# A transformer block on one core: eight PSUM banks and early feed-forward tiles in the epilogue, an earlier norm, halved stores and four banks of maxima in the prologue

## Chip, cores and metric

The kernel runs on one NeuronCore of one Trainium2 chip. The metric is the device time of one execution in microseconds; lower is better. Names used below: PE is TensorE, ACT is ScalarE, DVE is VectorE, POOL is GpSimd, SP is the SyncE queue that issues nearly all DMAs. A bank is one of the eight 128x512 fp32 accumulators in PSUM.

## What is computed

Eight batches of 1024 tokens with 256 channels go through one adaptive-norm transformer block: causal attention with 16 heads of 16 channels, then a feed-forward layer with a router over four low-rank experts (top two). Cut to what matters:

```
mod = (silu(c) @ wmod).reshape(8, 6, 1, 256);  sa, ca, ga, sb, cb, gb = mod[:, 0..5]
h = layernorm(x) * (1 + ca) + sa
x = x + ga * attention(h)          # q, k, v, o: x @ w.T + x @ a.T @ b.T / 16
h = layernorm(x) * (1 + cb) + sb
w, top = router(h)                 # softmax of h @ Wg.T + bg, the two best of four experts
hid_e = relu(h @ Wi.T + low_rank_e(h))              # 1024 hidden channels
x = x + gb * sum over the two experts of w_e * (hid_e @ Wo.T)
```

## The kernel before

Each engine walks one common plan, a list of steps in one order (`walk`, line 352), and issues its own part of each step. So the plan's order is the order of every engine's queue, and of SP's DMAs. The plan has phases: `prologue_plan` (line 258: weights turned, batch 0 normalised and projected, maxima of its first head group), eight bodies (`body_plan`: attention of batch i, with the feed-forward work of batch i-1 and the projections of batch i+1 laid between), and `epilogue_plan` (line 277: output projection, second norm, route and feed-forward of the last batch, with no attention beside it).

PSUM is divided by use: three `dense` banks, two `mxs` banks for the maxima, two `st` banks for scores, one `ov` bank for the attention output. Steps in `DENSE` take the dense banks in turn.

The steps that matter here:

- `su i`: setup. `su 0` to `su 8` make the modulation and the four projection matrices; `su 3` on DVE is `setup_gates` (line 1141); `su 9` to `su 18` turn the feed-forward weights.
- `ls1`/`ln1` and `ls2`/`ln2`: statistics (line 1159) and normalisation (lines 1181 to 1194, then 1294) of the first and the second norm, all on DVE. `t1`/`t2`: PE turns the result, ACT applies the modulation (line 1085).
- `pa`/`pj`: a projection of q or k in two matmul steps; ACT, DVE and POOL split it into three bf16 parts (lines 1094, 1331, 1334, 751). `va`/`vp`/`vs`: values and their store.
- `ps ot`: SP stores the parts of q and k of one half of the channels to DRAM (line 636). `rs slot half g`: SP loads one head group's stack from there, 13 small DMAs (lines 646, 651). It waits for `ps`.
- `mx`: PE makes scores for the row maxima in an `mxs` bank (lines 880, 884), DVE reduces it (line 1314); PE waits for the bank used two steps before. The prologue has 39 `mx` steps, four beside each `su`. `ms`, `nm`: the maxima are finished, turned by PE (line 972), copied by ACT (line 1109), and put into the stack by DMA (line 672); then the first scores `qk` (line 896) can start.
- `oa`/`op`: output projection (line 849), gated by DVE (line 1353), added to x by POOL (line 763).
- `rt`, `rx`, `ro`: route: logits, turn, `lg` copy by DVE (line 1359), then a chain of small DVE instructions (lines 1220 to 1262). `mt`, `rb` (lines 967, 861): its results are turned by PE and copied by ACT to `low_st` (1105) and `ratio_b` (1107).
- `fa`, `fx`, `fb`: one of 16 feed-forward tiles (half of the tokens, eighth of the hidden channels): base product (two 128x512 fp32 products on line 855, the first in `fa`, the second in `fx`), low-rank part of the best expert (line 922), relu by ACT (line 1079), then in the same bank the difference to the second expert (line 928), DVE (line 1368, two buffers `second`), POOL adds the two into `hid` (line 756). `wa`/`w`: the output product over `hid` (lines 1001, 936), DVE (1377), POOL (769), SP stores the rows. `w` of the first token tile waits for the last tiles of `hid`.

In the epilogue before, the order of the tiles is fa, fx, fa, fx, fb, fb for each pair.

## Time and profile before

| | us |
|---|---|
| median of 3 runs | 1964.28 (1963.49 to 1966.62) |
| the profiled execution | 1965.01 |
| its span in the trace | 1963.3 |
| PE busy | 1801.6 (92% of the span) |
| DVE busy | 1239.0 (63%) |
| ACT busy | 939.6 (48%) |
| POOL busy | 530.5 (27%) |

How to read it: the span is what the trace covers; 1.7 us of the execution lie outside it. Times of rows count from the span's start. The body runs from about 101 to 1850 us; what is before it is the prologue, what is behind it the epilogue. A busy PE is not a PE at full rate: its clock has two levels, and the column PEclk gives the granted one as a share of 2.4 GHz.

### The profile page before, as it was taken

The page shows a single profiled execution, that of the slowest core. Times are in us where ns is not written, and L with a number is a line of the kernel's source. Part 1 is how long each engine was busy: PE and PEld are TensorE (multiplying, and loading weights), DVE is VectorE, ACT ScalarE, POOL GpSimd, SP SyncE. Part 2 cuts the span into 40 slices and gives each one's busy share as a digit, 9 for nine tenths or more (in the row PEclk, how much of TensorE's full clock was granted, in tenths as well). Part 3 has the DMA queues.
Part 4 walks back from the last instruction along what each step waited for, and adds up shares of the span by engine and source line. Part 5 has one row for each costly group of instructions (what it writes and reads, how often), then busy time and mean ns, then how long its engine had stood idle before and what let it go on. Part 6 is the DMA issues. An engine that isn't in the chain of part 4 may idle for free. (4 is left out here: it accounts for less than half of the span.)

```text
span 1963.3 us, 31621 instructions
## 1 busy us (share of the span) xinstructions
PE 1801.6 (92%) x10868; PEld 943.5 (48%) x10868; DVE 1239.0 (63%) x2681; ACT 939.6 (48%) x1701; POOL 530.5 (27%) x833
## 2 busy tenths in 40 slices
PE   7689879999989999899999999899999999799868
PEld 5334335454544555444554545445554545344535
DVE  3666677757686577666676576765777565863131
ACT  2145555544455445545455445554455454554320
POOL 2012112233223222233222232232222332133313
PEclk9579899999999999999999999999999999899979
DMA  7523243213322223223222233223222132120000
GB/s 177 145 50 87 51 87 83 70 40 78 85 60 71 56 64 87 70 38 92 63 71 70 40 85 70 72 58 82 47 60 79 31 88 63 39 39 25 25 1 22
DMA packets 249862, 128.69 MB, mean 66 GB/s; under 512 B 158214, under 2 KB 244834, under 8 KB 249708
## 3 DMA queue, kind: packets, MB, share of 16 engines
q1 hardware_dynamic: 245564, 125.61, 26.6%
q10 hardware_dynamic: 4144, 1.07, 0.4%
q8 instruction: 92, 1.51, 0.4%
q14 instruction: 62, 0.51, 0.1%
HBM read 83.06 MB, written 41.97 MB: 64 GB/s over the span
## 5 line engine op out<-in xcount | busy, mean ns | idle before, releaser
L1049 ACT ACTIVATE probs<-st 128x512 f32<-128x512 f32 (+1 forms) x1216 | 674.8, 576 | 705.2 <-PE st L896 703.1
L1314 DVE TENSOR_REDUCE negm<-mxs 128x1 f32<-128x384 f32 (+4 forms) x736 | 446.6, 617 | 243.3 <-PE mxs L884 239.1
L896 PE MATMUL st<-q_st,k_st 98*128 98x512 bf16 (+3 forms) x1536 | 452.3, 333 | 25.5 <-ACT probs L1049 18.3
L880 PE MATMUL mxs<-k_st,q_st 96*128 96x512 bf16 (+3 forms) x1280 | 408.1, 329 | 47.0 <-DVE negm_left L1314 26.7
L1314 DVE TENSOR_REDUCE negm_left<-mxs 128x1 f32<-128x512 f32 x512 | 345.2, 687 | 144.6 <-PE mxs L880 142.2
L911 PE MATMUL ov<-probs,v_g 128*32 128x512 f32 (+3 forms) x3072 | 333.2, 506 | 1.2 <-POOL probs L743 1.1
L880 PEld LDWEIGHTS mxs<-k_st,q_st 96*128 96x128 bf16 x1280 | 124.0, 98 | 300.8 <-DVE negm_left L1314 98.6
L855 PE MATMUL dense<-c_t,wi_t 128*128 128x512 f32 x512 | 263.9, 601 | 3.3 <-ACT ratio_b L1107 2.4
L756 POOL TENSOR_TENSOR hid<-hid,second 128x512 f32<-128x512 f32 x128 | 161.7, 1266 | 305.6 <-DVE second L1368 305.6
L896 PEld LDWEIGHTS st<-q_st,k_st 98*128 98x128 bf16 x1536 | 142.3, 99 | 169.1 <-ACT probs L1049 66.1
L740 POOL TENSOR_TENSOR fence<-fence 128x1 f32<-128x1 f32 x256 | 50.2, 196 | 613.8 <-ACT probs L1049 613.7
L884 PE MATMUL mxs<-k_st,q_st 128*128 128x128 bf16 x1024 | 188.8, 225 | 14.9 <-DMA k_st<-k_parts_scratch 9.1
L1368 DVE SCALAR_TENSOR_TENSOR second<-dense,ratio_b 128x512 f32<-128x512 f32 x128 | 88.3, 690 | 135.8 <-PE dense L928 135.8
L743 POOL TENSOR_SCALAR_AFFINE_SELECT probs<-probs 128x512 f32<-128x512 f32 x256 | 162.5, 635 | 0.0
L884 PEld LDWEIGHTS mxs<-k_st,q_st 128*128 128x128 bf16 x1024 | 93.6, 100 | 90.6 <-issue 25.3
L841 PE MATMUL dense<-h_t,w_t 128*128 128x512 f32 x256 | 134.1, 613 | 1.1 <-ACT v_rows L1097 0.8
L911 PEld LDWEIGHTS ov<-probs,v_g 128*32 128x32 f32 x3072 | 61.0, 108 | 132.7 <-issue 98.8
L1079 ACT ACTIVATE hid<-dense 128x512 f32<-128x512 f32 x128 | 76.4, 597 | 96.0 <-PE dense L922 94.3
L936 PE MATMUL dense<-wo_t,hid 128*128 128x256 f32 x512 | 121.3, 379 | 0.0
L1001 PE MATMUL dense<-wo_t,hid 128*128 128x256 f32 x512 | 121.0, 379 | 0.0
L769 POOL TENSOR_TENSOR ob<-ob,x 128x256 f32<-128x256 f32 x64 | 47.1, 737 | 237.3 <-DVE ob L1377 237.3
L855 PEld LDWEIGHTS dense<-c_t,wi_t 128*128 128x128 f32 x512 | 89.3, 191 | 33.3 <-issue 20.1
(165 smaller groups left out, 1696.4 us busy)
## 6 DMA issues: line engine op xcount, KB each, us to landing
q_st<-q_parts_scratch SPq DMA_DIRECT2D x384, 64.0 KB
k_st<-k_parts_scratch SPq DMA_DIRECT2D x384, 64.0 KB
q_parts_scratch<-q_part SPq DMA_DIRECT2D x16, 768.0 KB, 3.3
k_parts_scratch<-k_part SPq DMA_DIRECT2D x16, 768.0 KB, 5.2
xin<-in_L_attn_x SPq DMA_DIRECT2D x8, 1024.0 KB, 5.9
values_scratch<-v_rows SPq DMA_DIRECT2D x32, 256.0 KB, 2.1
v_g<-values_scratch SPq DMA_DIRECT2D x128, 64.0 KB, 3.9
x<-in_L_attn_x SPq DMA_DIRECT2D x16, 512.0 KB, 4.3
```

The costliest lines, as they stand in the source:

```text
L743: nc.gpsimd.affine_select(out=tri, in_=tri, compare_op=ALU.is_ge, fill=0.0, base=0, pattern=[[0, HG], [1, P]], channel_multiplier=-1).then ...
L756: nc.gpsimd.tensor_tensor(hid[:, ft, :], hid[:, ft, :], second[:, ft % 2, :], ALU.add).then_inc(hid_ready, 1)
L841: return nc.tensor.matmul(db[:, :], w_t[:, WNAMES.index(which), k, ot * P:(ot + 1) * P], h_t[:, k, half * HB:(half + 1) * HB], start=(k == ...
L855: nc.tensor.matmul(db[:, :], wi_t[:, k, ft * P:(ft + 1) * P], c_t[:, k, half * HB:(half + 1) * HB], start=(k == 0), stop=False)
L880: last = nc.tensor.matmul(mxs[:, bank_m, j * n:j * n + left], q_st[0:KS, slot, h0 + j, qt * P:(qt + 1) * P], k_st[0:KS, slot, h0 + j, k0:k ...
L884: last = nc.tensor.matmul(mxs[:, bank_m, j * n + left:(j + 1) * n], q_st[:, slot, h0 + j, qt * P:(qt + 1) * P], k_st[:, slot, h0 + j, qt * ...
L896: last = nc.tensor.matmul(st[:, score_bank(ch, kt, h0), j * n:(j + 1) * n], k_st[0:KS + 2, slot, h0 + j, kt * P:(kt + 1) * P], q_st[0:KS + ...
L911: last = nc.tensor.matmul(ov[32 * j:32 * j + 32, HB - n:HB], v_g[:, slot, kt, j, :], probs[:, par, j, 0:n], start=(kt == 0), stop=(kt == 4 ...
L936: last = nc.tensor.matmul(db[:, 0:D], hid[:, ft, t * P:(t + 1) * P], wo_t[:, ft, :], start=False, stop=(ft == FT - 1))
L1001: nc.tensor.matmul(db[:, 0:D], hid[:, ft, t * P:(t + 1) * P], wo_t[:, ft, :], start=(ft == 0), stop=False)
L1049: nc.scalar.activation(probs[:, par, h0:h0 + heads, 0:n], st[:, score_bank(ch, kt, h0), 0:heads * n].rearrange("p (j q) -> p j q", q=n), A ...
L1314: nc.vector.tensor_reduce(dst[:, h0:h0 + heads], src, axis=AX.X, op=ALU.max, negate=True).then_inc(max_free, 1)
```

## The change

In the epilogue:

- The dense steps rotate over all eight banks instead of three; the first step waits until the last scores, maxima and output are read.
- For the last batch `fa` makes both base products, and five tiles' `fa` (`EARLY_TILES`) stand behind the route's steps and ahead of `mt`. After them each tile's `fa` follows the `fb` of the tile five before it, `fb` follows the `fx` of the tile two after it, and the first `fa` steps of the second token half stand ahead of the first half's `wa`.
- `ls2 i` follows `op i` directly, instead of all four following all four.

In the prologue:

- `ls1` and `ln1` follow `su 0`; the scale for `t1` is copied in `setup_gates` and ACT waits for that copy.
- `ps` is halved along the tokens everywhere (in the bodies the two halves follow each other). In the prologue the first half is stored as soon as its two projections are split, and the loads of the first group (`rs 0 0`, `rs 0 1`) come ahead of values 2 and 3 and their stores.
- `mx` uses four banks (`mxs` and `st`) instead of two.
- The second `ps` stands behind `nm 0` instead of ahead of it.

```diff
+    plan = [("su", 0)] + chain_steps(("ls1", "ln1")) + [("su", i) for i in range(1, N_PROJECTION_SETUP)]
+    plan += [("t1", i) for i in range(4)] + [("xin",)]
     values = [opened("va", i) for i in range(4)]
-    plan += values[0] + values[1] + pj[0] + [("ps", 0, 0)]
-    plan += values[2] + values[3] + [("rs", g, half, g) for g in range(2) for half in range(2)] + [("vg", 0)]
+    plan += values[0] + values[1]
+    for half in range(2):
+        plan += pj[0][4 * half:4 * half + 4] + [("ps", 0, 0, half)]
+    plan += [("rs", 0, half, 0) for half in range(2)] + values[2] + values[3]
+    plan += [("rs", 1, half, 1) for half in range(2)] + [("vg", 0)]
...
-    plan += [("ms",), ("ps", 1, 0), ("nm", 0)] + score_steps(0, *UNITS[0])
+    plan += [("ms",), ("nm", 0), ("ps", 1, 0, 0), ("ps", 1, 0, 1)] + score_steps(0, *UNITS[0])
...
 def epilogue_plan():
-    plan += [s for i in range(4) for s in opened("oa", i)]
-    plan += chain_steps(("ls2", "ln2")) + [("t2", i) for i in range(4)] + [("rt",), ("rx",)] + chain_steps(("ro",))
+    for i in range(4):
+        plan += opened("oa", i) + [("ls2", i)]
+    plan += chain_steps(("ln2",)) + [("t2", i) for i in range(4)] + [("rt",), ("rx",)] + chain_steps(("ro",))
+    tiles = [(half, ft) for half in range(2) for ft in range(8)]
+    plan += [("fa", *t) for t in tiles[:EARLY_TILES]]
     plan += [("mt", v) for v in range(2)] + [("rb", half) for half in range(2)]
     for half in range(2):
-        for ft in range(0, 8, 2):
-            plan += [(name, half, ft + i) for i in range(2) for name in ("fa", "fx")]
-            plan += [("fb", half, ft + i) for i in range(2)]
+        of_half = tiles[8 * half:8 * half + 8]
+        for i, t in enumerate(of_half):
+            plan.append(("fx", *t))
+            n = 8 * half + i - 2
+            if i >= 2:
+                plan.append(("fb", *tiles[n]))
+            if i >= 2 and n + EARLY_TILES < 16:
+                plan.append(("fa", *tiles[n + EARLY_TILES]))
+        for n in (8 * half + 6, 8 * half + 7):
+            plan.append(("fb", *tiles[n]))
+            if n + EARLY_TILES < 16:
+                plan.append(("fa", *tiles[n + EARLY_TILES]))
         plan += [s for t in range(4) for s in opened("wa", half, t)]
+EARLY_TILES = 5
+EPILOGUE_BANKS = 8
...
+        banks = [dense[:, i, :] for i in range(DENSE_BANKS)] + [mxs[:, i, :] for i in range(MAX_BANKS)]
+        banks += [st[:, i, :] for i in range(SCORE_BANKS)] + [ov[:, :]]
+        def max_room(it):
+            spare = [st[:, i, :] for i in range(SCORE_BANKS)] if it < 0 else []
+            return [mxs[:, i, :] for i in range(MAX_BANKS)] + spare
...
-                    ot, later = a
+                    ot, later, half = a
+                    cols = slice(half * HB, (half + 1) * HB)
                     for dst, src in ((q_d, q_part), (k_d, k_part)):
-                        sp.dma_start(dst[ot], src[:, ot, :, :]).then_inc(parts_out[ot], 16)
+                        sp.dma_start(dst[ot, :, :, cols], src[:, ot, :, cols]).then_inc(parts_out[ot][half], 16)
...
-                    sp.wait_ge(parts_out[ot], done(f"ps{ot}") * (2 * 16))
+                    sp.wait_ge(parts_out[ot][half], done(f"ps{ot}{half}") * (2 * 16))
...
-                    after(pe, max_free, done("mx") - MAX_BANKS + 1)
+                    room = max_room(it)
+                    out = room[done("mx") % len(room)]
+                    after(pe, max_free, done("mx") - len(room) + 1)
...
                     elif kind == "fa":
                         hidden(db, 0, *a)
+                        if it == NB:
+                            hidden(db, 1, *a)
                         return
```

## Rows read from the trace of the kernel before

**Rows 1.** Busy time of each engine by stage, then granted clock, DMA share, GB/s
```profile
62.66:94.40 31.74, 26.17 (x110) 13.73 (x110) 24.89 (x41) 5.31 (x9) 1.15 (x1) 0.50 0.56 129
...
100.89:1850.47 1749.58, 1645.82 (x10211) 843.15 (x10211) 1156.16 (x2471) 898.34 (x1633) 481.14 (x764) 0.98 0.27 64
...
1861.94:1887.64 25.70, 6.51 (x35) 4.14 (x35) 15.65 (x67) 3.71 (x6) 1.72 (x2) 0.60 0.00 0
```

**Rows 2.** Timeline of the prologue ahead of the first maxima: start, duration, engine, line
```profile
30.76 1.50 PE L861 MATMUL dense<-ident,xin 128*128 128x128 f32 x12 [0.66 <-DVE xin L1294]
...
43.66 1.15 POOL L751 TENSOR_TENSOR k_part<-rest,k_part 128x512 bf16<-128x512 f32 x1 [0.55 <-DVE k_part L1334]
...
48.66 0.43 SPq L636 DMA_DIRECT2D k_parts_scratch<-k_part  x1
...
53.56 0.73 SPq L646 DMA_DIRECT2D q_st<-blank_scratch  x1
...
62.66 0.61 PE L884 MATMUL mxs<-k_st,q_st 128*128 128x128 bf16 x4 [6.70 <-DMA k_st<-k_parts_scratch]
```

**Rows 3.** The first load of `xin`, issued at 1.74 us: from issue to landing
```profile
DMA to landing us min/median/max: 9.1/9.1/9.1
```

**Rows 4.** DVE's longest group of waits in the maxima: total us, times, longest
```profile
DVE negm L1314 <- PE mxs L884: 8.2, 7, 5.1
```

**Rows 5.** Timeline of the first scores
```profile
100.89 1.03 PE L896 MATMUL st<-q_st,k_st 98*128 98x512 bf16 x2 [4.70 <-DMA q_st<-m_row]
```

**Rows 6.** SP's timeline in the first body: a store, and the next load
```profile
179.76 0.43 SPq L636 DMA_DIRECT2D k_parts_scratch<-k_part  x1
187.82 0.62 SPq L646 DMA_DIRECT2D q_st<-blank_scratch  x1
```

**Rows 7.** Timeline of the epilogue, output projection and second norm
```profile
1856.87 0.69 DVE L1353 TENSOR_TENSOR second<-dense,gates_b 128x512 f32<-128x512 f32 x1 [5.02 <-PE dense L849]
1857.71 1.27 POOL L763 TENSOR_TENSOR x<-x,second 128x512 f32<-128x512 f32 x1 [8.60 <-DVE second L1353]
...
1864.16 2.71 DVE L1159 BATCH_NORM_STATS2 stats<-x 128x6 f32<-128x256 f32 x8 [1.44 <-POOL x L763]
```

**Rows 8.** Timeline of the epilogue around the route
```profile
1879.93 0.39 DVE L1359 COPY lg<-dense 128x80 f32<-128x80 f32 x2 [7.04 <-PE dense L991]
...
1887.64 1.91 PE L967 MATMUL dense<-ident_b,low_w 128*96 128x128 bf16 x16 [7.75 <-DVE low_w L1262]
1888.74 1.92 ACT L1105 COPY low_st<-dense 96x1024 bf16<-96x1024 bf16 x2 [7.43 <-PE dense L967]
...
1890.55 1.25 ACT L1107 COPY ratio_b<-dense 128x512 f32<-128x512 f32 x2
```

**Rows 9.** Short stretches where the granted clock falls and rises, columns as in rows 1
```profile
58.00:58.50 0.50, 0.00 (x0) 0.00 (x0) 0.24 (x2) 0.00 (x0) 0.00 (x0) 0.50 0.49 148
...
1887.60:1891.00 3.40, 3.36 (x24) 3.25 (x24) 0.00 (x0) 2.26 (x3) 0.00 (x0) 0.51 0.00 0
1891.00:1894.40 3.40, 2.63 (x9) 1.17 (x8) 0.00 (x0) 0.98 (x3) 0.00 (x0) 1.00 0.02 5
```

**Rows 10.** The chain that ended last, one pair of tiles: start, duration
```profile
1930.92 1.72 PE dense L855 x4
1932.64 0.22 PE dense L922
...
1934.83 0.61 ACT hid L1079
```

**Rows 11.** Timeline of the same pair of tiles, and of the last output rows
```profile
1935.49 0.39 PE L928 MATMUL dense<-low_st,b_stack 96*128 96x512 bf16 x1 [0.47 <-ACT hid L1079]
...
1935.82 2.49 POOL L756 TENSOR_TENSOR hid<-hid,second 128x512 f32<-128x512 f32 x2 [2.46 <-DVE second L1368]
1935.91 0.69 DVE L1368 SCALAR_TENSOR_TENSOR second<-dense,ratio_b 128x512 f32<-128x512 f32 x1 [0.17 <-PE dense L928]
...
1959.81 0.48 DVE L1377 SCALAR_TENSOR_TENSOR ob<-dense,rs_,gates_b 128x256 f32<-128x256 f32 x1 [2.97 <-PE dense L936]
```

74 lines of the change are left out of this document (44 added, 30 removed).

## Prediction, made before the changed kernel was run

> **What bounds the kernel now.** I read the busy time by stage first. In the body PE is busy for 1645.8 of 1749.6 us at a granted clock of 0.98 [rows 1]: it is the bound there, and the change removes no PE work from it. So whatever the change brings must come from the 100 us ahead of the body and the 113 us behind it. Four stretches there leave PE waiting. First, PE stands 6.7 us until the first stack has landed [rows 2]. Second, the maxima take 31.74 us, in which DVE works for 24.89 and PE runs at clock 0.50 [rows 1]. Third, between the output projection and the route's result PE works 6.5 of 25.7 us [rows 1]. Fourth, the feed-forward of the last batch, some 68 us, is a chain of PE with one exposed relu per pair of tiles [rows 10, 11].
>
> **Prologue, start of the loads.** Before, the loads began at 53.56, because SP stored q and k only after both halves were split (issue of k at 48.66) and waited for the landing [rows 2]. Now the first half can be stored when its k is split, 43.66 + 1.15 = 44.8. The early norm takes some more: the load of xin landed at 1.74 + 9.1 = 10.8 [rows 3], the norm's DVE work is 8.7 us (the epilogue's twin of it runs from 1864.16 to 1872.9), so it ends near 20, long before the turns at 29.5. What it saves is only the wait of 0.66 [rows 2] less what ACT then can't follow: I take 0.5. So the first half is issued by 45.1. But SP still has the second half's store in its queue ahead of the loads: that waits for POOL as before, 0.5 earlier, and its two issues end at 49.09 - 0.5 = 48.6. The first half has landed by then if it takes 3.5 us, and by 50.0 if it takes as long as the whole took from 48.66 (4.9, up to 53.56). I take 48.6, as half the bytes move: loads 4.9 us earlier (bound 3.5). From the first load to the first max it was 62.66 - 53.56 = 9.1 us, 13 issues and a landing, and stays so: first max at 57.7. PE's own work before it ends at 55.5 and doesn't hold it. The stores of values 2 and 3 go behind these loads on SP; they are needed by the gather `vg`, whose queue turn comes after all four loads, near 76, and by the product at about 96. Cost nothing.
>
> **Prologue, the maxima.** With two banks PE may be one step ahead of DVE, so each `su` between them (four turns, 0.86 us at the half clock) starves DVE: its largest group of waits is 8.2 us, of which 5.1 is the start [rows 4], and 31.74 - 24.89 = 6.9 us of the stage are without DVE [rows 1]. With four banks, a replay of the order by hand (a 512-column product 0.43 us of PE, a reduce 0.67, 0.54 or 0.40 of DVE, DVE 0.3 behind PE) never starves DVE after the start. The stage is then DVE's 24.9 us plus 0.7 at the start plus 0.6 for gaps, 26.2: 5.5 us shorter. The bounds: DVE without any gap gives 6.1. If the second half's stack comes late (its loads end at 61.4, land at 64.1, PE wants it at about 64.6) or PE at 0.50 is the slower (its 26.2 busy us [rows 1], run in series, with the start), 3. Behind the maxima, turn, copy and the row's DMA are as before; the first scores stay bound to that DMA [rows 5]. The second store now stands behind it, lands near 95 and is first loaded in unit 7, some 40 us later. Prologue: -4.9 - 5.5 = **-10.4 us**, between -12 and -6.5. The body starts on the same work, just earlier.
>
> **Body.** 14 stores become pairs of halves: two more issues each of 0.34 to 0.43 us, 0.8 us of SP, and runs of 1 KB where they were longer. The load behind such a store began 7.6 us after its issue ended (180.19 to 187.82), against a landing of about 5 from its start [rows 2, 6]: some 3 us of slack hide it. Taken as 0; below nothing is excluded only for the store itself, since where PE's clock dips fall in the body moves with the start; I allow +-2 for that.
>
> **Epilogue, the second norm.** Here the change costs. DVE's queue is in order: `ls2 i` waits for POOL's sum, and the next `op` stands behind it. One link is 0.69 (DVE) + 0.15 + 1.27 (POOL) + 0.03 + 2.71/4 (statistics) = 2.84 us [rows 7]. Four make 11.4 from 1856.87, so statistics end at 1868.2, against 1864.16 + 2.71 = 1866.9 before: **+1.4 us**, and everything up to the route is that much later. Eight banks give nothing back here, since no dense step waited for a bank.
>
> **Epilogue, the filled gap.** `fa` of tile 0 needs all banks read, so it follows the `lg` copy: 1880.32 + 0.1 + 1.4 = 1881.8. The route's last result comes at 1887.6 + 1.4 = 1889.0 [rows 8]. Five tiles at 1.72 us [rows 10] are 8.6 us at full clock. But PE stands at 0.50 here, and rose 3.3 us after it had become continuously busy [rows 9]: 3.3 us at half speed add 1.7, twice that 3.3. I take 2.5: `fa` ends at 1881.8 + 11.1 = 1892.9, 3.9 us after the route, so the turns start later than before by 5.3. From their start, ACT is the chain: 0.6 for the first turn at full clock, copies of 1.92 and 1.25 [rows 8], 0.1: the first `fx` starts at 1896.8, against 1890.55 + 1.25 + 0.1 [rows 8] + 1.72 = 1893.7 before: **+3.1 us** (this holds the +1.4). At once at full clock it would be +0.6, at half clock for all five (17.2 us) +9.2.
>
> **Epilogue, from the first `fx` to the end.** Before: 1893.7 to 1959.81, 66.1 us [rows 11]. It held 15 base products, now 11: -4 x 1.72 = -6.9. One pair of tiles showed relu 0.61 and its handover, with PE idle 0.47 and 0.17 more of refilling [rows 10, 11]: 8 x 0.64 = -5.1. What comes back: `fb 0` of each half stands too close to its relu (2 x 0.42), and at the end of the second half no base products are left between the tiles, so PE needs 0.44 per tile (two low-rank products at 0.22 [rows 10]), ACT 0.61, DVE 0.69 and POOL 1.25 (2.49 for two) [rows 11]. There PE waits 0.4 twice for relus; the last five tiles queue at POOL, and the first `w` waits 0.15 + 0.76 + 1.62 for `hid`. Together +4.1. Sum **-7.9 us**. In the first half base products of the second lie in between, and POOL keeps up. The tail behind the last `w` is unchanged. Epilogue: +3.1 - 7.9 = **-4.8**.
>
> **The sum.** -10.4 - 4.8 = -15.2. Against the profiled execution 1965.0 - 15.2 = 1949.8; against the median, which lies 0.7 below it, **1949.1 us**.
>
> **The rivals.** (A) The clock takes the fill back. PE keeps 0.50 through all five `fa`: +6.1, 1955.2. For it: in the 25.7 us around the norm and the route PE works in pieces and gets 0.60 on average [rows 1]. Against: its `fa` are gapless, as the work was before the rise. A milder form is that the clock falls between the last `fa` and the first `fx`: 1.7 us of turns and 2.2 us of waiting; PE is at 0.50 from 58.0, and its last instruction before the 6.7 us of waiting for the stack [rows 2] had ended at 62.66 - 6.70 = 55.96, so it fell after 2.0 us [rows 9]. It would then stay low some 3.3 us and cost 1.7: 1950.8. The Trainium skill speaks for this form ("TensorE: Matmul & The Clock Gate", Part 4, PE-mode transpose): transposes do not count as PE-busy, so the whole 3.9 us would be idle to the clock. The trace speaks against that page: from 1887.6 to 1891 PE did turns only, 3.36 of 3.40 us, and the clock rose at the end of it [rows 9]. (B) The prologue gives half: the loads start when they did, since the halved stores share the queues and land late, or the maxima become bound by PE or by the second half's stack. 1949.1 + 4.9 = 1954.0 or + 2.5 = 1951.6; both 1956.5. For it: the slack at the second half's stack is 0.5 us. (C) Slower: the halved stores in the body. Each of the 14 loses its slack when it lands over 7.6 us after the issue, and then PE, the bound, waits for the loads behind it. At 9 us each costs 1.4: +19.6, 1968.7, slower. It decides from a landing of about 9 us; against it, the bytes are the same and SP is idle for long. (D) More than forecast: fill at full clock at once (-2.5) and an earlier rise in the first body, 1945.
>
> **Chances and range.** Forecast 0.60 (1946 to 1953); A 0.12; B 0.15; C 0.04; D 0.06; the prologue or the fill not doing what it says while the other does, near 1960, 0.03. Low end: D with a shorter prologue, 1944.5. High end: B whole, 1956.5; that leaves out under 2 in 10. About 0.2% (3.9 us) is what a measurement of this kernel tells from no change: faster 0.91, within it 0.05, slower 0.04.
>
> **What would show it.** Right: first load near 48.6 and first max near 57.7; no reduce waiting over 0.3 us after the start and `ms` near 84; first scores near 90.5; statistics of the second norm 11.4 us behind the first `op`; five tiles of line-855 products between the `lg` copy and the turns, the first two at half rate; no relu wait inside the first half; POOL back to back at the end of the second half, with PE waiting for it some 2.5 us at the first `w`. Wrong: the stage of the maxima near 30 us; a granted clock of 0.50 over all `fa`; a body whose length differs from 1749.6 by over 2 us; loads that wait for halved stores.

## The result, and the profile of the changed kernel

The changed kernel took 1948.01 us (median; 1945.34 to 1949.17 in four runs) beside 1965.45 us for the kernel before on the same chip. The ratio is 0.9895 with a 95% interval of 0.987 to 0.9921. Measured twice more, it came to 0.9905 (0.9883 to 0.9927) and 0.9894 (0.9871 to 0.9917). So the change is faster by some 1.0%, where 15.2 us or 0.8% were forecast, and the time fell in the range. All three intervals lie below 1. The profiled execution took 1949.06 us with a span of 1947.3, that is 16.0 us less span.

The stages first, as in rows 1: the maxima, the body, the stretch from the end of norm 2's statistics to the route's end, and the last piece of the five early tiles.

```profile
57.70:82.17 24.47, 18.58 (x110) 10.71 (x110) 23.20 (x41) 5.32 (x9) 1.15 (x1) 0.79 0.70 129
88.50:1837.70 1749.20, 1646.19 (x10210) 844.25 (x10211) 1155.78 (x2471) 898.92 (x1633) 481.08 (x764) 0.98 0.28 65
1859.25:1878.85 19.60, 12.46 (x47) 7.05 (x48) 12.20 (x58) 3.71 (x6) 0.00 (x0) 0.68 0.00 0
1878.85:1882.10 3.25, 3.25 (x9) 1.27 (x8) 0.00 (x0) 0.00 (x0) 0.00 (x0) 1.00 0.00 0
```

The body is what it was: 1749.20 us against 1749.58, PE busy 1646.19 against 1645.82 [rows 1]. The maxima are 7.3 us shorter and DVE now works in 23.20 of 24.47 us. Everything that was gained lies ahead of the first scores (12.4 us) and behind the body (3.2 us in this profile). The rest of the 16.0 is the body's 0.4.

Next the timeline of the prologue (start, duration, engine, line), the rows that answer to rows 2 and rows 5. L920 is the first maximum, L932 the first score.

```profile
28.05 2.18 PE L893 MATMUL dense<-ident,xin 128*128 128x128 f32 x16
...
43.52 0.62 SPq L668 DMA_DIRECT2D k_parts_scratch<-k_part  x1
...
46.26 0.51 SPq L668 DMA_DIRECT2D q_parts_scratch<-q_part  x1
46.82 0.63 SPq L668 DMA_DIRECT2D k_parts_scratch<-k_part  x1
47.56 0.73 SPq L678 DMA_DIRECT2D q_st<-blank_scratch  x1
...
52.40 1.83 SPq L683 DMA_DIRECT2D q_st<-q_parts_scratch  x1
...
57.70 0.40 PE L920 MATMUL mxs<-k_st,q_st 128*128 128x128 bf16 x4 [3.75 <-DMA k_st<-k_parts_scratch]
...
88.50 1.04 PE L932 MATMUL st<-q_st,k_st 98*128 98x512 bf16 x2 [4.67 <-DMA q_st<-m_row]
```

The first half's store ends its issue at 44.14 and the loads begin at 47.56, 0.11 us behind the second half's last issue. The first half had landed just before. This is the view of `k_parts_scratch` from 40 to 60 us; the longest, 4.0 us from the issue at 43.52, is the first half's k:

```profile
DMA to landing us min/median/max: 3.4/3.7/4.0
```

So it landed at 47.5, and here landing and queue let the loads go at practically the same moment. In the two other profiles of this kernel it had landed 0.04 and 0.11 us before the last issue ended. The turns of norm 1 no longer have a gap in front of them. One of the small load issues took 1.83 us where its neighbours take 0.43.

The waits in the stage of the maxima (total, times, longest), which answer to rows 4: DVE waits for 2.0 us at the start and once more for 0.6, at 66.8 us.

```profile
DVE negm L1360 <- PE mxs L920: 2.0, 1, 2.0
DVE negm_left L1360 <- PE mxs L916: 0.6, 1, 0.6
```

Then the epilogue: one link of the second norm, the base products behind the `lg` copy, the turns of `mt`, and the end of the second half.

```profile
1850.78 0.67 DVE L1399 TENSOR_TENSOR second<-dense,gates_b 128x512 f32<-128x512 f32 x1
1851.59 1.26 POOL L795 TENSOR_TENSOR x<-x,second 128x512 f32<-128x512 f32 x1 [1.52 <-DVE second L1399]
1852.89 0.75 DVE L1204 BATCH_NORM_STATS2 stats<-x 128x6 f32<-128x256 f32 x2 [1.44 <-POOL x L795]
1853.56 0.67 DVE L1399 TENSOR_TENSOR second<-dense,gates_b 128x512 f32<-128x512 f32 x1
...
1871.75 5.36 PE L887 MATMUL dense<-c_t,wi_t 128*128 128x512 f32 x8 [0.48 <-DVE lg L1405]
1876.95 3.60 PE L887 MATMUL mxs<-c_t,wi_t 128*128 128x512 f32 x8
1880.38 1.88 PE L887 MATMUL st<-c_t,wi_t 128*128 128x512 f32 x4
1882.10 0.61 PE L1007 MATMUL st<-ident_b,low_w 128*96 128x128 bf16 x8
...
1926.07 6.16 POOL L788 TENSOR_TENSOR hid<-hid,second 128x512 f32<-128x512 f32 x5 [0.89 <-DVE second L1414]
...
1927.48 1.97 PE L1043 MATMUL mxs<-wo_t,hid 128*128 128x256 f32 x8 [0.37 <-POOL hid L788]
1929.85 1.13 PE L976 MATMUL mxs<-wo_t,hid 128*128 128x256 f32 x4 [0.40 <-POOL hid L788]
1932.29 1.13 PE L976 MATMUL mxs<-wo_t,hid 128*128 128x256 f32 x4 [1.31 <-POOL hid L788]
```

DVE's queue shows the new chain: a statistics step waits 1.44 us for POOL, and the next `op` starts only as it ends, every 2.78 us. The base products fill the route; the first eight take 5.36 us where the next eight take 3.60, because the clock rose inside them. At the end five adds stand back to back at POOL and PE waits 0.37 + 0.40 + 1.31 = 2.08 us for them.

### The profile page after: what moved, and what is told of

It is laid out like the page before. It is cut to its first block, busy times and chain, and to the rows that moved or that the text cites. A ratio compares the mean times of both kernels' runs of the same rounds, so it can differ in the third digit from the quotient of the medians.

```text
span 1947.3 us, 31669 instructions
## 1 busy us (share of the span) xinstructions
PE 1795.9 (92%) x10868; PEld 943.3 (48%) x10868; DVE 1236.8 (64%) x2681; ACT 939.5 (48%) x1701; POOL 530.6 (27%) x833
## 3 DMA queue, kind: packets, MB, share of 16 engines
q10 hardware_dynamic: 4144, 1.07, 0.4%
## 4 chain that ended last, share of the span: by engine, by line
PE 75%; DVE 14%; ACT 4%; issue 3%; SPq 2%; DMA 1%; POOL 1%; POOLq 0%; DVEq 0%; ACTq 0%
PE ov L947 12%; PE st L932 10%; PE dense L887 10%; PE mxs L916 9%; PE dense L873 5%; PE dense L1043 5%; PE dense L976 5%; PE dense L881 4%; DVE negm L1360 4%; PE dense L893 3%; DVE negm_left L1360 3%; PE mxs L920 2%; PE dense L968 2%; ACT probs L1091 1%; SPq L683 1%
## 5 line engine op out<-in xcount | busy, mean ns | idle before, releaser
L1360 DVE TENSOR_REDUCE negm<-mxs 128x1 f32<-128x384 f32 (+4 forms) x725 | 439.7, 617 | 238.2 <-PE mxs L920 234.5
L932 PE MATMUL st<-q_st,k_st 98*128 98x512 bf16 (+3 forms) x1536 | 454.2, 334 | 25.7 <-ACT probs L1091 17.3
L916 PE MATMUL mxs<-k_st,q_st 96*128 96x384 bf16 (+2 forms) x1261 | 397.6, 325 | 44.1 <-DVE negm_left L1360 26.2
L1360 DVE TENSOR_REDUCE negm_left<-mxs 128x1 f32<-128x512 f32 x504 | 339.5, 686 | 140.7 <-PE mxs L916 138.8
L887 PE MATMUL dense<-c_t,wi_t 128*128 128x512 f32 x480 | 250.4, 606 | 3.0 <-ACT ratio_b L1151 1.7
L932 PEld LDWEIGHTS st<-q_st,k_st 98*128 98x128 bf16 x1536 | 142.2, 99 | 169.4 <-ACT probs L1091 65.5
L920 PE MATMUL mxs<-k_st,q_st 128*128 128x128 bf16 x1009 | 184.4, 224 | 11.3 <-DMA k_st<-k_parts_scratch 5.5
L1414 DVE SCALAR_TENSOR_TENSOR second<-dense,ratio_b 128x512 f32<-128x512 f32 x120 | 82.8, 690 | 117.1 <-PE dense L968 115.2
L920 PEld LDWEIGHTS mxs<-k_st,q_st 128*128 128x128 bf16 x1009 | 91.4, 99 | 87.6 <-issue 25.7
L801 POOL TENSOR_TENSOR ob<-ob,x 128x256 f32<-128x256 f32 x64 | 47.1, 737 | 239.3 <-DVE ob L1423 239.3
L1043 PE MATMUL dense<-wo_t,hid 128*128 128x256 f32 x464 | 109.6, 379 | 0.0
L976 PE MATMUL dense<-wo_t,hid 128*128 128x256 f32 x464 | 109.6, 379 | 0.0
L1121 ACT ACTIVATE hid<-dense 128x512 f32<-128x512 f32 x120 | 71.3, 597 | 76.7 <-PE dense L962 75.0
L887 PEld LDWEIGHTS dense<-c_t,wi_t 128*128 128x128 f32 x480 | 84.0, 192 | 28.1 <-issue 14.0
```

The costliest lines, as they stand in the source:

```text
L887: nc.tensor.matmul(db[:, :], wi_t[:, k, ft * P:(ft + 1) * P], c_t[:, k, half * HB:(half + 1) * HB], start=(k == 0), stop=False)
L916: last = nc.tensor.matmul(out[:, j * n:j * n + left], q_st[0:KS, slot, h0 + j, qt * P:(qt + 1) * P], k_st[0:KS, slot, h0 + j, k0:k0 + left ...
L920: last = nc.tensor.matmul(out[:, j * n + left:(j + 1) * n], q_st[:, slot, h0 + j, qt * P:(qt + 1) * P], k_st[:, slot, h0 + j, qt * P:(qt + ...
L932: last = nc.tensor.matmul(st[:, score_bank(ch, kt, h0), j * n:(j + 1) * n], k_st[0:KS + 2, slot, h0 + j, kt * P:(kt + 1) * P], q_st[0:KS + ...
L976: last = nc.tensor.matmul(db[:, 0:D], hid[:, ft, t * P:(t + 1) * P], wo_t[:, ft, :], start=False, stop=(ft == FT - 1))
L1043: nc.tensor.matmul(db[:, 0:D], hid[:, ft, t * P:(t + 1) * P], wo_t[:, ft, :], start=(ft == 0), stop=False)
```

## Experiments

The stages in the profiles of the kernel before and of the changed kernel, profiled three times, in us (starts are of the first instruction; "ce" is the epilogue's first turn; "last DVE step" is the start of DVE's last instruction):

| | before | changed | again | once more |
|---|---|---|---|---|
| first value projection | 33.64 | 31.63 | 31.14 | 31.41 |
| first load | 53.56 | 47.56 | 47.07 | 47.34 |
| load to first max | 9.11 | 10.15 | 10.06 | 10.65 |
| maxima | 31.73 | 24.47 | 23.76 | 24.43 |
| first scores | 100.89 | 88.50 | 86.95 | 88.88 |
| body | 1749.58 | 1749.20 | 1750.04 | 1748.33 |
| ce to first `op` | 6.40 | 10.26 | 6.46 | 10.26 |
| first `op` to end of statistics | 10.01 | 11.24 | 11.24 | 11.25 |
| statistics to end of `lg` | 13.44 | 12.49 | 12.50 | 12.49 |
| route's end to turns | 0.15 | 3.28 | 3.31 | 3.27 |
| turns to first `fx` | 6.09 | 3.79 | 3.79 | 3.79 |
| first `fx` to last DVE step | 66.07 | 57.93 | 57.93 | 57.92 |

### One half of the change at a time

`e1_epilogue_only` has the old order of the prologue, with two banks for the maxima, and the new epilogue; its stores stay halved, both halves next to each other. `e2_prologue_only` is the reverse.

```diff
 # e1_epilogue_only
-    plan = [("su", 0)] + chain_steps(("ls1", "ln1")) + [("su", i) for i in range(1, N_PROJECTION_SETUP)]
+    plan = [("su", i) for i in range(N_PROJECTION_SETUP)]
+    plan += chain_steps(("ls1", "ln1")) + [("t1", i) for i in range(4)] + [("xin",)]
...
-            spare = [st[:, i, :] for i in range(SCORE_BANKS)] if it < 0 else []
+            spare = []
...
 # e2_prologue_only
-    plan += [("fa", *t) for t in tiles[:EARLY_TILES]]
...
-    phase(epilogue_plan(), batches, EPILOGUE_BANKS)
+    phase(epilogue_plan(), batches)
```

> The changed epilogue with the prologue's order, two banks of maxima and the late norm as before; stores stay halved, both halves next to each other. Theory 1 (the two ends add up, each worth what its stages show): first load near 53 to 54, first max to the end of the maxima 31 to 32 us, and from the first turn of the epilogue (ce) to the end 109.6 us if the clock dips there again, near 106 if it does not, against 112.8 before. Time 3 to 7 us below the kernel before, 1958 to 1962. Theory 2 (the halved stores alone start the prologue's loads earlier, whatever the order): first load below 52. Theory 3 (the gain at the end is spent on the longer norm and the late turns): from ce to the end 112 or more, time as before.

> The changed prologue with the epilogue as before (three banks, pairs of tiles, statistics after all four gated rows). Theory 1: first scores near 88.5 to 90.5 against 100.9, body 1749 to 1750 long, from ce to the end 112.8; time 10.4 to 12.4 below before, 1953 to 1955. Theory 2 (an earlier start is lost again in the body, whose pace is set by something else): body longer than 1752, time above 1956.

Measured: the epilogue alone 1960.98 us, ratio 0.9965 (0.995 to 0.9979); the prologue alone 1954.52 us, 0.9927 (0.9907 to 0.9946), beside 1968.89 for before. That is 7.9 and 14.4 us. The two together give 1.08%, the whole change 0.95 to 1.06%: within the intervals the halves add up. The prologue carries about two thirds, as forecast. Both medians are where Theory 1 had them. The profiles agree: `e1` has its first load at 54.01 and 107.33 us from ce to the end, against 112.81 before; `e2` has its first scores at 88.28 and a body of 1750.01 us. Only its epilogue took 116.72 us where 112.8 were expected, 3.8 of it at its first turns (last section). Theory 2 of `e1` (halving alone starts the loads earlier) is out: there the first half's k had landed at 52.6, but SP was still issuing the stores of values until 53.9.

### The statistics behind the projection

```diff
-    for i in range(4):
-        plan += opened("oa", i) + [("ls2", i)]
-    plan += chain_steps(("ln2",)) + [("t2", i) for i in range(4)] + ...
+    plan += [s for i in range(4) for s in opened("oa", i)]
+    plan += chain_steps(("ls2", "ln2")) + [("t2", i) for i in range(4)] + ...
```

> The changed kernel with one edit undone: the statistics of the second norm come after all four gated rows again. Theory 1 (statistics between the rows make DVE wait for POOL four times in series): from the first gated row to the last statistics 10.0 us instead of 11.2, and all behind it 1.2 us earlier; time 1 to 1.5 below the changed kernel. Rival (the oa rows or PE are the later ones, so the order does not matter): no difference in that stretch. Rival 2 (statistics between rows save, as meant): the stretch becomes longer than 11.2.

> The changed kernel once more, for the phase of TensorE's clock. Theory 1 (the half clock at the epilogue's first turns, 3.9 us longer from ce to the first gated row than before, is chance): here that stretch (10.3 us in the first profile, 6.4 before) may come out at 6.4 again, and the setup turns L834 at 273 or 421 ns each. Rival (the change causes it): 10.3 again. Ratio to before 0.987 to 0.992.

Measured: 1947.65 us, 0.9894 (0.9874 to 0.9914), beside 1947.63 for the changed kernel. (That one took 6.46 us from ce to the first `op` this time, so its Theory 1, chance, held; see the last section.) Its stage shrank to 10.00 us as it had been before (11.24 in the changed kernel): in this stage the new order costs 1.24 us, and DVE's statistics now run as one block.

```profile
1848.72 1.26 POOL L794 TENSOR_TENSOR x<-x,second 128x512 f32<-128x512 f32 x1 [0.46 <-DVE second L1398]
1850.01 2.71 DVE L1203 BATCH_NORM_STATS2 stats<-x 128x6 f32<-128x256 f32 x8 [1.44 <-POOL x L794]
```

But the total didn't move; the 1 to 1.5 us that were expected didn't come. (The profiled execution, 1944.06 us, is the shortest of its six, by a body of 1745.42 us, and isn't a measure of the edit.) The windows of this kernel from the statistics to the `lg` copy, and from there on:

```profile
1852.72:1866.33 13.61, 6.47 (x34) 4.10 (x34) 5.92 (x34) 3.48 (x5) 0.00 (x0) 0.50 0.00 1
1866.33:1876.00 9.67, 9.61 (x18) 4.33 (x19) 6.33 (x26) 0.23 (x1) 0.00 (x0) 0.79 0.00 0
```

The clock stayed at 0.50 through the turns and logits (13.61 us against 12.50), and the turns of `mt` began 3.63 us after the route instead of 3.31. So 1.24 us came off and 1.11 + 0.32 came back through the clock. From the first `op` to the first `fx` this kernel takes 38.16 us and the changed one 37.92. That is no accident of this one profile: the three kernels with the statistics in one block and no products added (before, `e2`, `e3`) have 13.44, 13.45 and 13.61 us from the statistics to the end of `lg`, while all seven profiles with the statistics between the rows and no products added (the changed kernel three times, `e1`, `e4`, `e5`, `e6`) have 12.36 to 12.50. In those the logits already run at the high clock and take 1.07 us instead of 1.93. Whether the order itself brings the clock's rise forward isn't shown, since no run moves the clock alone.

### Two banks for the maxima, and the stores in one piece

```diff
 # e4_two_max_banks
-            spare = [st[:, i, :] for i in range(SCORE_BANKS)] if it < 0 else []
+            spare = []
 # e5_stores_together
-    for half in range(2):
-        plan += pj[0][4 * half:4 * half + 4] + [("ps", 0, 0, half)]
+    plan += pj[0] + [("ps", 0, 0, 0), ("ps", 0, 0, 1)]
```

> The changed kernel with two banks for the prologue's maxima instead of four. Theory 1 (PE may be only one step ahead, so each setup step starves DVE): first max to end of maxima back to 31 to 32 us at the half clock, 28 if part of it runs at full clock, against 24.5 and 23.8 in the two profiles of the changed kernel; DVE waits for PE some 5 us more. Rival (the stage became short because the clock stayed full at its start, since the stack came earlier): 24 to 26 us here too.

> The changed kernel with both halves of the first store put behind all four projections of the first half of the channels, loads directly behind them. Theory 1 (the loads' start is the second half's store issue, because the landing of the first half is hidden behind it): loads start when the second half has landed, so from the first value projection to the first load 19.5 to 20 us instead of 15.9, first max 3.5 to 4 later, time 3.5 to 4 above the changed kernel. Rival (SP's queue order alone, the loads ahead of the values' stores, made the gain): 16 to 17 us.

Measured with two banks: 1955.97 us, 0.994 (0.9922 to 0.9959). The stage of the maxima:

```profile
58.33:90.06 31.73, 26.17 (x110) 13.72 (x110) 24.88 (x41) 5.31 (x9) 1.15 (x1) 0.50 0.50 100
```

It is the stage of before to 0.02 us in each engine [rows 1], as Theory 1 had it; the rival (24 to 26 us here too) is out. The profiled execution is the longest of the ten (1966.47 us), but for reasons behind this stage: its body took 1758.73 us. The two banks more are worth 31.73 - 24.47 = 7.3 us and the other edits of the prologue nothing here. The granted clock was higher with four banks too (0.79 for 0.50), and PE's busy time follows it (18.58 against 26.17). How much of the 7.3 belongs to that isn't separated, since all three profiles with two banks (before, `e1`, `e4`) had 0.50 throughout. With four banks the granted clock lay between 0.74 and 0.86 and the stage between 23.8 and 24.5 us, and DVE was busy for 23.20 of the 24.47 us: in that range PE's rate hardly sets the length.

Measured with the stores together: 1952.4 us, 0.9929 (0.9905 to 0.9952). SP's queue in this kernel:

```profile
48.15 0.65 SPq L667 DMA_DIRECT2D q_parts_scratch<-q_part  x1
48.84 1.09 SPq L667 DMA_DIRECT2D k_parts_scratch<-k_part  x1
50.94 0.73 SPq L677 DMA_DIRECT2D q_st<-blank_scratch  x1
```

From the first value projection to the first load it was 18.77 us, against 15.93 in the changed kernel in every profile. So the early store of the first half is worth 2.84 us at the load's start. Only 1.0 us of SP's queue is idle here (49.93 to 50.94). The wait is for the first half, whose k was issued at 47.49 and landed at 50.92, 3.4 us later, where the whole of before had taken 4.9. The second half landed only at 53.19. So Theory 1 was wrong in what the loads wait for, and 18.77 lies between its 19.5 to 20 and the rival's 16 to 17. Against the kernel before (19.92) the other 1.15 us is mostly the faster landing of a half. It doesn't come by halving alone: `e1`, with the values' stores in front of the loads, has 20.13.

### Three tiles open in the second half

The order lets the second half keep only three tiles' base products ahead, so that two base products more lie among the last tiles.

```diff
     for half in range(2):
...
-            if i >= 2 and n + EARLY_TILES < 16:
-                plan.append(("fa", *tiles[n + EARLY_TILES]))
...
+        ahead = EARLY_TILES if half == 0 else LATE_AHEAD
+        limit = 8 + LATE_AHEAD if half == 0 else 16
...
+            if name == "fb" and begun < limit and begun <= n + ahead:
+                plan.append(("fa", *tiles[begun]))
+                begun += 1
...
 EARLY_TILES = 5
+LATE_AHEAD = 3
```

> The changed kernel with a shorter lead in the second token half: only three of its tiles' base products are made during the first half, the other five lie between its tiles. Same PE work. Theory 1 (the last tiles queue at POOL, 1.25 us each, because no base product lies between them): PE's waits for hid and relu at the first output product fall from about 3.1 to 1.7 us, first fx to last output row 57.0 us against 57.9. Rival (PE waits there for something else): 57.9 or more.

Measured: 1946.18 us, 0.9892 (0.9865 to 0.9919); first `fx` to last DVE step 57.16 us, against 57.93. POOL's block and the wait of the first `w`:

```profile
1926.52 3.71 POOL L794 TENSOR_TENSOR hid<-hid,second 128x512 f32<-128x512 f32 x3 [0.89 <-DVE second L1420]
1930.29 1.13 PE L982 MATMUL st<-wo_t,hid 128*128 128x256 f32 x4 [1.12 <-POOL hid L794]
```

Three adds in a block instead of five, and PE waits once for 1.12 us instead of three times for 2.08. In return PE now waits 0.55 us at the first half's `w`, where two tiles begun early had stood before. The stretch is 0.8 us shorter, as expected (57.0 for 57.9), so the queue at POOL behind the last tiles is shown as a cost; the medians (1946.18 here, 1947.6 to 1948.5 for the changed kernel) can't tell.

### Extra products ahead of norm 2's turns

```diff
+WARM = 11
...
+                    if it == NB and step == ("t2", 0):
+                        after(pe, dense_free[bank], done(f"bank{bank}"))
+                        for i in range(WARM):
+                            nc.tensor.matmul(db[:, :], w_t[:, 0, i % KC, 0:P], h_t[:, i % KC, 0:HB],
+                                             start=True, stop=True)
```

> The changed kernel with eleven 128x512 fp32 products added on PE, whose results nobody reads, while DVE normalises ahead of t2. Theory 1 (the half clock in t2, the route and the five early fa costs some 3 us): the clock stays at 1.0 from the gated rows to the end; last statistics to the lg copy 11.5 us against 12.5 (13.5 where the clock rose late); route's end to the turns 1.5 us against 3.3; turns to first fx 3.8 as before; together 2.5 to 3 us shorter from the last statistics to the first fx (was 26.7). Rival (a mere DVE and ACT chain, PE's rate does not matter): 26 to 27. If the products outlast the norm, the first stretch grows instead.

Measured: 1944.84 us, 0.9886 (0.9863 to 0.9908). From the statistics to the first `fx` it took 24.2 us, against 26.7 in the changed kernel: 11.67 us to the end of `lg` instead of 12.49, and the turns 1.62 us after the route instead of 3.28. So far Theory 1 held. Four windows from the turns of `mt` on:

```profile
1879.32:1883.12 3.80, 2.16 (x26) 1.71 (x25) 0.00 (x0) 2.89 (x4) 0.00 (x0) 1.00 0.00 0
1883.12:1884.90 1.78, 1.52 (x6) 0.64 (x7) 0.29 (x1) 1.37 (x3) 0.00 (x0) 1.00 0.00 0
1885.00:1888.30 3.30, 3.30 (x7) 1.21 (x6) 0.30 (x1) 0.44 (x2) 1.26 (x1) 0.50 0.00 0
1888.40:1942.73 54.33, 51.75 (x194) 33.75 (x193) 13.65 (x22) 6.89 (x13) 23.86 (x22) 1.00 0.05 17
```

Here the milder form of rival A happened: after 3.80 us in which PE worked 2.16, the clock fell for 3.4 us, and first `fx` to last DVE step took 59.62 us instead of 57.93. That is the 1.7 us that the rival had named, and of the 2.5 us won 0.8 are left: from the first `op` to the last DVE step it is 95.08 us against 95.85. `e1` and `e4` show the fall as well (both 59.62, both with the turns 1.6 us behind the route), and there the two cancel: 95.91 and 95.89 us. Those where the turns came 3.0 us or more behind the route don't show it; there the clock had risen later, in the early tiles themselves. One kernel further down (`e9`) has the turns at 1.6 and no fall, so this isn't a rule.

### All together, with four tiles and with five

`e8_best` joins four edits: statistics behind the projection, three tiles open in the second half, nine extra products, and four tiles begun early. `e9_five_open` is the same with five early tiles and eleven products.

```diff
 # e9_five_open against e8_best
-WARM = 9
-EARLY_TILES = 4
+WARM = 11
+EARLY_TILES = 5
 LATE_AHEAD = 3
```

> Four edits to the changed kernel at once: four FFN tiles begun ahead of the route's end instead of five, three tiles held open at a time in the second half instead of five, norm 2's statistics all behind the output projection, and nine extra 128x512 products (work without use) ahead of norm 2's turns, to bring the clock up earlier. My theory: by the earlier runs' stages the statistics take 10.0 us from the first output projection (not 11.24), statistics to logits 11.7 (not 12.5), route end to turns 0.2 (not 3.3, as four tiles at full clock end within the route), turns to first fx 3.8, first fx to last DVE step 58.0 (57.2 for the POOL queue relieved, or 59.6 with the clock falling once more between the last fa and the first fx, mean near 58.0 to 58.9): in all 4 to 5 us under the changed kernel where the clock is in the same phase at the epilogue's start, 1942 to 1945 us, ratio to before near 0.987. Rival: the clock gives it back, since PE at full clock idles more in the route and the granted clock falls for a longer stretch at the first low-rank products: then first fx to last DVE step is 61 or more and the time is that of the changed kernel, 1946 to 1950. The difference that is asked for is a quarter of a per cent, so the stages of the profile decide more than the median.

> The changed kernel a third time, on the chip of the run beside it. All theories expect 1945 to 1950 us (ratio 0.989 to 0.992), the maxima in 24 to 25 us and first fx to last DVE step 57.9; what may differ is where the clock falls: the time from the first turn of the context to the first output projection is either near 6.5 or near 10.2 us, and in the two profiles of this kernel so far it was once each.

> The last kernel with five tiles begun early instead of four and eleven extra products instead of nine; the other two edits (three tiles open in the second half, the statistics behind the output projection) stand. My theory, from the stages of the runs before: with four tiles PE waited 0.78 us four times in the first half for a bank that DVE hadn't freed, with five it doesn't, so first fx to last DVE step is 57.2 us, or 58.9 where the clock falls once more between the last fa and the first fx; statistics 10.0 us, statistics to logits 11.7 to 12.9, route end to turns 1.6. The epilogue from the first turn of the context to the end then takes 102 us where the clock is high there and 106 where it falls, 3 to 4 under the changed kernel in the same phase, and the median is 1943 to 1946 us, ratio near 0.988. Rival: the time that these edits save on DVE and in the start of the clock is idle time for PE, and the granted clock falls for it later; then first fx to last DVE step is 61 or more, as in the run with four tiles less its 3.4 us of waits (60.3), and the median is that of the changed kernel, 1947 to 1949.

Measured with four: 1953.5 us, 0.9913 (0.9888 to 0.9938), no faster than the changed kernel beside it (1948.53) and by the medians slower. The expected 1942 to 1945 was wrong, and the rival's cause only in part right. The turns came 1.95 us behind the route instead of 0.2, because the clock stood at 0.50 from 1867.3 to 1877.6, into the early tiles. First `fx` to last DVE step took 63.73 us. The clock fell for 3.4 us, as in the run before; the rest is in PE's timeline:

```profile
1891.75 0.38 PE L974 MATMUL dense<-low_st,b_stack 96*128 96x512 bf16 x1
1892.91 1.98 PE L893 MATMUL dense<-c_t,wi_t 128*128 128x512 f32 x4 [0.78 <-DVE second L1425]
...
1894.95 0.38 PE L974 MATMUL mxs<-low_st,b_stack 96*128 96x512 bf16 x1
1896.11 1.98 PE L893 MATMUL mxs<-c_t,wi_t 128*128 128x512 f32 x4 [0.78 <-DVE second L1425]
```

With four tiles open the next `fa` stands right behind the `fb` whose bank it takes, and it waits for DVE to read that bank. This came four times in the first half, once at the half clock. At full clock each costs 1.05 us: `fb` to `fa` took 1.16 us from start to start where it takes 0.21 without the wait, and the products 1.82 for 1.72. Against `e6` (57.16) the first wait, with the fall of the clock in it, adds 2.5 us and the three others 3.2. One tile less begun early also leaves one tile's base products more in this stretch, 1.72 us, and the wait of 0.55 at the first half's `w` is gone; so the 6.6 us are accounted for to within 0.3. I had counted neither: my rule for the number of early tiles looked only at the route's end.

It isn't that banks had run out. The steps take the eight banks in turn. Tile 0 to 3, the two turns `mt` and the two copies `rb` are eight steps, so the ninth, `fa` of tile 4, comes back to the bank of tile 0, which `fb` has just written, and the three after it likewise. The four banks of `mt` and `rb` had been read before the first `fx`. With five tiles the count is one off, and `fa` of tile 5 takes a bank of `mt`. So what cost the time was which bank was next, not how many were free; a rotation that skips to a free bank wasn't tried.

Measured with five: 1942.4 us (1939.83 to 1950.32), beside 1969.86 for before, 0.9872 (0.9849 to 0.9896). It is the fastest kernel of the study, a little below the 1943 to 1946 that were expected. Its two windows from ce to the first `fx` and on to the last DVE step, and behind them those of the changed kernel:

```profile
1836.78:1877.45 40.67, 33.60 (x153) 20.25 (x154) 18.40 (x72) 8.44 (x14) 5.07 (x4) 1.00 0.04 13
1877.45:1934.61 57.16, 54.67 (x204) 35.26 (x204) 14.26 (x24) 9.12 (x16) 25.19 (x23) 1.00 0.05 16
```

```profile
1837.70:1885.89 48.19, 31.57 (x130) 21.33 (x131) 18.41 (x72) 8.94 (x14) 5.05 (x4) 0.75 0.03 11
1885.89:1943.82 57.93, 55.09 (x204) 35.31 (x204) 14.37 (x24) 8.91 (x16) 25.12 (x23) 1.00 0.05 16
```

Of the 8.3 us between them, 3.8 are the place at which the clock stands at the first turns (below), which no edit of mine has shown to govern. The other 4.5 are stages with an edit behind them: 1.2 in the statistics, 0.8 to the end of `lg`, 1.7 behind the route, 0.8 at POOL. Against the changed kernel the ratios differ by 0.22 points of a per cent, some 4.3 us, but their intervals overlap. So the stages, not the medians, carry the claim. The rival (the clock takes it back later) didn't happen in this profile: the granted clock was 1.00 throughout. But 1.7 of the 4.5 us hang on that, since in `e7`, with the same products added, the clock did fall once more and took them back. The profiled execution is the shortest of the six (up to 1950.32); what the clock did in the others isn't known.

## Why the prediction was right, and where a term was off

**The bound.** Right. The body kept its 1749.2 us, halved stores and all; over the other profiles of kernels with halved stores it lay between 1745.4 and 1752.1 (1758.7 in one whose clock stood at 0.50 up to 124.9 us). Rival C, the stores landing late, isn't seen in them: in the changed kernel's body a store's last piece had landed at least 2.1 us before the load behind it began, where before it was 3.3. So some of the slack went, and none of the loads waited.

**Start of the loads.** Forecast 48.6, in the three profiles 47.1 to 47.6, so 6.0 us gained in the first of them instead of 4.9 (first load 53.56 before). The mechanism held: the first half's landing and the end of SP's queue fell within 0.11 us of each other. The landing took 4.0 us from the issue of k where I had allowed 3.5, but the queue's end was 3.9 us behind that issue too, and in the first profile the landing was the later of the two by 0.07 us. Within that, one term was mis-sized: the early norm, taken at 0.5. The first value projection came 2.0 us earlier. `e1` shows why. It has the late norm and, by chance, the full clock in setup, and PE waits for DVE's `xin` twice there:

```profile
29.71 0.63 PE L890 MATMUL dense<-ident,xin 128*128 128x128 f32 x4 [1.27 <-DVE xin L1336]
31.01 1.50 PE L890 MATMUL dense<-ident,xin 128*128 128x128 f32 x12 [0.67 <-DVE xin L1336]
```

In the profile of before the 16 small turns of `su 3` and `su 4` took 3.02 us, against 2.10 in `e1` and 1.99 in the changed kernel. So PE came to `t1` later, and what was left of the wait was the 0.66 of rows 2. I had read it off one execution, in which a slow PE hid most of it. The change of order alone was not run, so this is read from profiles of kernels that differ in more. Like against like, the early norm is worth 33.88 - 31.63 = 2.2 us where those turns are quick, and 33.64 - 32.59 = 1.0 where they are slow (`e6`). The store's own part, value projection to load, went from 19.92 to 15.93, so 4.0 where 4.4 had been taken.

**First load to first max.** Taken as 9.1 and unchanged; it was 10.1 to 10.7 in the changed kernel, where one of the issues took 1.83 us. The 13 issues took 8.18 us from first to last where they had taken 6.32, and from there to the first max it was 1.96 us for 2.78. The long issue isn't rare: of the eleven profiles with these loads ahead of the values' stores nine have one of 1.7 to 2.1 us, `e5` one of 1.16 and `e9` one of 0.92. In before and `e1` no issue of these 13 took over 0.8. So it comes with the change, and a term that stood at nothing cost about 1 us. Why one issue takes so long isn't shown. With it the first max came at 57.70, the very time forecast, which is luck: errors of opposite sign cancelled.

**The maxima.** The mechanism was right: one DVE wait of 0.6 us is left behind the start, where there had been eight of 0.5 to 0.6, and `e4` puts the whole of it on the banks. (The sign I had named, no wait over 0.3 us, was too strict.) The size was off by 1.7 us (24.5 for 26.2, 7.3 gained for 5.5). I had replayed the order with PE at 0.50 and a reduce every 0.67 us. What ran had the granted clock at 0.79, and reduces back to back take less each. Here are two rows of before and three of the changed kernel (start, duration, and how many are in the row):

```profile
73.78 2.09 DVE L1314 TENSOR_REDUCE negm_left<-mxs 128x1 f32<-128x512 f32 x3 [0.59 <-PE mxs L880]
77.05 2.69 DVE L1314 TENSOR_REDUCE negm_left<-mxs 128x1 f32<-128x512 f32 x4 [0.59 <-PE mxs L880]
```

```profile
69.36 1.29 DVE L1360 TENSOR_REDUCE negm_left<-mxs 128x1 f32<-128x512 f32 x2
70.56 1.28 DVE L1360 TENSOR_REDUCE negm_left<-st 128x1 f32<-128x512 f32 x2
71.76 1.01 DVE L1360 TENSOR_REDUCE negm<-mxs 128x2 f32<-128x512 f32 x2
```

In the changed kernel four 512-column reduces start in 2.40 us, one every 0.60, while each lasts 0.68: they overlap by 0.08. The kernel before shows three in 2.09, one every 0.70, behind a wait: there too some neighbours start 0.61 apart, but others 0.79, with no overlap. Over the stage the durations of DVE's 41 instructions add up to nearly the same, 26.31 us before and 26.13 in the changed kernel, while the time with DVE busy, in which an overlap counts once, fell from 24.89 to 23.20. So my bound "DVE without any gap" (24.9 us) was no bound: busy time shrinks when instructions stand closer.

**The second norm.** 2.84 us a link was forecast, 2.78 measured; +1.4 forecast, +1.24 measured, and `e3` takes just that away. In this stage it is a cost of the change, named as such. Up to the first `fx` it isn't: with the new order `lg` came sooner after the statistics, in every profile (see `e3`).

**The filled gap.** The five tiles ended 3.3 us after the route, forecast 3.9: the clock rose 3.4 us after the first of them began, as in rows 9, and I had taken 2.5 us for the slow part where about 1.8 came (5.36 against 3.60 for the first eight products). But it had not stood at 0.50 until then, as I had it: it had risen during the logits and fell again as the first tile began. Two windows of the changed kernel:

```profile
1868.30:1871.70 3.40, 1.48 (x18) 0.70 (x18) 0.39 (x2) 1.04 (x2) 0.00 (x0) 1.00 0.00 0
1871.75:1875.10 3.35, 3.35 (x4) 1.51 (x5) 2.84 (x15) 0.23 (x1) 0.00 (x0) 0.50 0.00 0
```

From the turns to the first `fx` it took 3.79 us, forecast 3.9. Route's end to first `fx` is 7.07 us against 6.24 before. With the norm's 1.24, less the 0.95 by which `lg` came sooner after the statistics, that is +1.1 where +3.1 stood. That `lg` came sooner was again the clock (before 13.44, here 12.49). `e3`, which has the old order of the statistics, has 13.61, so this goes with the change, though why isn't shown; I had put it at nothing.

**The feed-forward.** Forecast -7.9, measured 66.07 - 57.93 = 8.1. Both parts that come back were in place: POOL's queue (2.08 us of waits forecast as 2.53) and short relu waits (0.26 us at the first `fb` of each half, forecast 0.42). `e6` confirms the first. Eight banks and early tiles were not run one without the other.

**The sum.** Forecast -10.4 and -4.8; by the profile -12.4 and -3.2, with 3.8 us of clock at the epilogue's start against the change in this profile (10.26 us for 6.40, ce to first `op`). Without that the epilogue would be -7.1, near the 7.9 us that `e1` gave in its median. So both halves gave 2 us more than forecast, and the clock took part of it back in the profile. In the ratios that shows as 1.0% for 0.8%. That the profiled time (1949.06) came within 1 us of the forecast for it (1949.8) is luck to that extent.

**The rivals.** A in its full form (all five tiles at half clock) was not seen. Its milder form was seen in four experiments, in three of them (`e1`, `e4`, `e7`) at its price of 1.7 us. B, half of the prologue, would have had the maxima at PE's pace; DVE's busy 23.20 of 24.47 us is against it. (Its price for that, a stage 3 us shorter, isn't what the row gives: PE's 26.2 us and 0.7 for the start would be 4.8 shorter.) D expected more by the fill and an earlier rise in the first body; what was gained beyond the forecast came from the prologue and the clock in the logits instead.

**The turns and the clock.** The Trainium skill ("TensorE: Matmul & The Clock Gate", Part 4, PE-mode transpose) says that transposes don't count as PE-busy in the same way. If they didn't count at all, the milder form would have been the rule. Of the nine kernels with early tiles it came in `e1`, `e4`, `e7` and `e8`, and not in the changed kernel (three profiles), `e3`, `e5`, `e6` and `e9`. PE does the same turns in all of them, and in `e7` and `e9` at the same distances, so the turns alone don't decide it. That the clock rose behind 3.4 us of turns alone [rows 9] speaks against their not counting at all. That they count for less is neither borne out nor excluded.

## What to carry to other kernels

Where a short stage alternates between two engines through a pair of banks and a third kind of work is laid between, more banks let the waiting engine run on what is ready; the gain is about the stage less the busy time of its slower engine (6.9 us here, 7.3 measured), and neighbouring instructions may overlap on top. When filling a gap with work begun early and taking banks in turn, write down which bank each step gets: if the turn comes round to the bank that was just written, each step of the loop pays (0.78 us of wait here), though other banks are free. Read a wait in more than one execution before taking its size, since an engine that happened to be slow hides it.

## What was not expected of the hardware

**The clock's place is a matter of the execution, and worth 3.8 us at one point.** The same kernel, profiled twice, from ce to the first `op`; the first is the changed kernel, the second the same again:

```profile
1837.70:1847.97 10.27, 8.60 (x30) 7.13 (x31) 0.69 (x3) 2.34 (x4) 0.00 (x0) 0.51 0.15 48
```

```profile
1837.00:1843.46 6.46, 4.63 (x30) 3.99 (x31) 0.68 (x2) 2.05 (x4) 0.00 (x0) 1.00 0.27 85
```

Same instructions, clock 0.51 and 1.00, 3.8 us. The low clock stood in the changed kernel, its third measurement, `e2`, `e4`, `e7` and `e8`; the high one in before, the changed kernel again, `e5`, `e6` and `e9`; `e1` and `e3` lay between (7.97). `e2` has the epilogue of before and the changed kernel has shown both, so the new epilogue doesn't decide it. What does wasn't found. A single profile of this kernel says nothing about edits under some 4 us unless they are read stage by stage, and, as `e3` shows, with the stages behind them added up.

**Load issues on SP are not even.** Most take 0.43 us, but the tenth of the first 13 took 1.72 to 2.09 us in nine of the eleven profiles with the new order, and in `e5` the sixth took 1.16. The first halved stores took 0.51 to 0.65 us each in the changed kernel, and up to 1.10 where two halves stood next to each other, where the whole ones had taken 0.34 and 0.43 [rows 2].
